# Moving the constant loads, the first bias addition and one group of scatters in an attention and mixture-of-experts kernel

## The reference

```
mod = (silu(c) @ wmod).reshape(4, 6, 1, 256); sa, ca, ga, sb, cb, gb = ...
h = layernorm(x) * (1 + ca) + sa
x = x + ga * attention(h)            # 16 heads of 16 channels, softmax over 1024 keys
h = layernorm(x) * (1 + cb) + sb
x = x + gb * ffn(h)                  # sigmoid gate, top 6 of 32 experts out of 4 of 8 groups,
                                     # silu(g) * u @ down per expert, plus one shared expert
```

## Time and profile before

| | us |
|---|---|
| median of 3 runs (lowest, highest) | 1454.37 (1452.69, 1455.62) |
| the profiled execution, its own time | 1454.37 |
| the profiled execution, span from first to last instruction | 1452.5 |
| attention with routing, about | 126 to 900 |
| TensorE busy | 1312.8 (90%) |
| VectorE busy | 1142.6 (79%) |
| GpSimd busy | 606.2 (42%) |

### The profile page before, as it was taken

One profiled execution on the slowest core, in us unless ns is written; L12 is line 12 of the kernel. 1 busy time (PEld: TensorE's weight loads), 2 busy tenths in 40 slices (PEclk: granted clock), 3 DMA queues, 4 the chain that ended last, 5 costly groups with the idle time before them and its releaser, 6 DMA issues.

```text
span 1452.5 us, 30593 instructions
## 1 busy us (share of the span) xinstructions
PE 1312.8 (90%) x8111; PEld 659.5 (45%) x8112; DVE 1142.6 (79%) x2793; ACT 754.2 (52%) x1155; POOL 606.2 (42%) x782
## 2 busy tenths in 40 slices
PE   7997999999999999999999998999999999999500
PEld 4552222333323323333233334657888888888400
DVE  7886999999999999999999972634666666566498
ACT  3772577767676676667676683103333333333100
POOL 4000123324634547346364477243555555555300
PEclk9997799999999999999999999999999999999855
DMA  6887355436345544465354647674555555555497
GB/s 219 262 267 189 114 164 131 103 82 135 99 118 151 130 109 105 116 160 125 88 127 136 185 130 222 213 236 125 175 178 172 180 179 169 181 176 171 167 418 299
DMA packets 216958, 243.52 MB, mean 168 GB/s; under 512 B 93949, under 2 KB 181501, under 8 KB 216738
## 3 DMA queue, kind: packets, MB, share of 16 engines
q1 hardware_dynamic: 187890, 164.78, 41.4%
q0 software_dynamic: 21776, 68.07, 13.1%
q10 hardware_dynamic: 7200, 9.51, 2.0%
HBM read 133.98 MB, written 108.28 MB: 167 GB/s over the span
## 4 chain that ended last, share of the span: by engine, by line
PE 68%; DVE 17%; DMA 3%; issue 1%; ACT 1%; SPq 1%; POOL 0%; DVEq 0%; POOLq 0%
PE ex_psGU L1620 14%; PE psO L1169 13%; PE psE L1156 12%; PE psM L1146 9%; DVE piece_max L1044 9%; PE ex_psY L1635 7%; PE ex_psX L1611 3%; PE psGU L1464 2%; PE psM L503 2%; PE psX L1475 2%; DVE wide L1758 2%; PE ex_psA L1629 2%; DVE wide L1760 2%; PE psM L522 1%; DVE wide L1761 1%
## 5 line engine op out<-in xcount | busy, mean ns | idle before, releaser
L1044 DVE TENSOR_REDUCE piece_max<-psM 128x1 f32<-128x512 f32 x1024 | 642.8, 682 | 26.4 <-PE psM L1146 22.9
L1110 ACT ACTIVATE wide<-psE 128x1024 f32<-128x1024 f32 x512 | 497.2, 1021 | 205.4 <-PE psE L1156 203.3
L1146 PE MATMUL psM<-wide 48*128 48x512 bf16 x1024 | 324.6, 395 | 19.7 <-DVE piece_max L1044 11.7
L1156 PE MATMUL psE<-wide 49*128 49x512 bf16 (+1 forms) x2048 | 330.1, 381 | 1.0 <-DMA wide<-maxima 0.5
L1704 POOL DMA_INDIRECT results<-vals_inv,places x223 | 213.7, 958 | 184.2 <-DVE vals_inv L1688 123.0
L1169 PE MATMUL psO<-wide 128*32 128x512 f32 x2048 | 274.0, 607 | 0.6 <-ACT wide L1110 0.6
L1146 PEld LDWEIGHTS psM<-wide 48*128 48x128 bf16 x1024 | 78.1, 93 | 348.0 <-DVE piece_max L1044 276.4
L1620 PE MATMUL ex_psGU<-wide,ex_xT 128*128 x892 | 231.8, 382 | 0.8 <-ACT ex_xT L1653 0.5
L1620 PEld LDWEIGHTS ex_psGU<-wide,ex_xT 128*128 128x128 f32 x892 | 152.0, 190 | 16.6 <-issue 4.6
L1156 PEld LDWEIGHTS psE<-wide 49*128 49x128 bf16 (+1 forms) x2048 | 117.7, 95 | 91.0 <-issue 9.4
L1653 ACT ACTIVATE ex_xT<-ex_psX 128x256 f32<-128x256 f32 x223 | 85.3, 383 | 122.9 <-PE ex_psX L1611 121.8
(11 more groups left out here) (240 smaller groups left out, 1222.0 us busy)
## 6 DMA issues: line engine op xcount, KB each, us to landing
wide<-qk_parts SPq DMA_DIRECT2D x384, 64.0 KB
wide<-results SPq DMA_DIRECT2D x16, 1536.0 KB, 10.5
rows<-lists SPq DMA_DIRECT2D x112, 160.0 KB, 2.2
last_rows<-lists SPq DMA_DIRECT2D x111, 160.0 KB, 2.7
qk_parts<-parts SPq DMA_DIRECT2D x32, 384.0 KB, 3.1
xin<-in_x_dram SPq DMA_DIRECT2D x16, 512.0 KB, 4.1
v_values<-vst SPq DMA_DIRECT2D x32, 256.0 KB, 3.6
wide<-v_values SPq DMA_DIRECT2D x16, 512.0 KB
```

Source lines behind the costliest of these rows:

```text
L1044: v.tensor_reduce(piece_max[:, qh, (x * PAIRS + h) * KT // QH + qt, kh:kh + 1], bank_of("piece", PIECES * group + n), AX.X, ALU.max, negat ...
L1110: nc.scalar.activation(probs[:, step % 2, 2 * pair:2 * pair + 2], psE[:, pair], ACT.Exp, scale=HD ** -0.5).then_inc(exp_ok, 1)
L1146: nc.tensor.matmul(bank_of(*user), qa[g][rows, h, qt * P:(qt + 1) * P], ka[g][rows, h, kh * 512:(kh + 1) * 512], start=True, stop=True).th ...
L1156: mm = nc.tensor.matmul(psE[:, pair, x], k[g][part, pair, kt * P:(kt + 1) * P], q[g][part, pair, qh * 512:(qh + 1) * 512], start=(q is qa) ...
```

## The change

There are three edits. On SP the constants and `load_x(0)` go ahead of the loop, and so ahead of `put_max(2)`. On GpSimd the wait for the constants, `scale_out(0)` and `add_bias(0)` go ahead of the 33 DMAs that fill the spare lists. In the odd chunks `add_bias(c + 1)` goes ahead of portion 2 of the scatters, as in the even ones.

```diff
@@ SP
             load_group(sp, env, 0, 3)
-            def load_constants():
-                for to, of in ((env.wo, env.woT), (env.gate_w, env.gateT), (env.wsg, env.wsgT), (env.wsd, env.wsdT)):
-                    sp.dma_start(to[:], of.rearrange("(k p) n -> p k n", p=P)).then_inc(const_in, 16)
-                sp.dma_start(env.bo_bc[:], env.bo_d.to_broadcast([P, D])).then_inc(const_in, 16)
-                sp.dma_start(env.ebias[:], env.ebias_d.to_broadcast([P, E])).then_inc(const_in, 16)
-
+            for to, of in ((env.wo, env.woT), (env.gate_w, env.gateT), (env.wsg, env.wsgT), (env.wsd, env.wsdT)):
+                sp.dma_start(to[:], of.rearrange("(k p) n -> p k n", p=P)).then_inc(const_in, 16)
+            sp.dma_start(env.bo_bc[:], env.bo_d.to_broadcast([P, D])).then_inc(const_in, 16)
+            sp.dma_start(env.ebias[:], env.ebias_d.to_broadcast([P, E])).then_inc(const_in, 16)
+            load_x(0)
...
                 if group + 1 < NGR:
                     put_max(2 * (group + 1))
-                if group == 0:
-                    load_constants()
-                    load_x(0)
                 if group % 2 == 0 and c >= 0:
                     load_x(c + 1)
@@ GpSimd
             pool.wait_ge(pads_built, 3)
+            pool.wait_ge(env.const_in, 16 * 6)
+            scale_out(0)
+            add_bias(0)
             spare = env.lists[E * CAP:LIST_ROWS].rearrange("(k p) n -> p k n", p=P)
             for k in range(E):
                 pool.wait_ge(summed, k + 1)
                 pool.dma_start(spare[:, k, 0:TARGET], env.pad_row[:, 0:TARGET]).then_inc(spare_in, 16)
             pool.dma_start(spare[:, :, TARGET:ROW], spare_to[:].bitcast(F32)).then_inc(spare_in, 16)
-            pool.wait_ge(env.const_in, 16 * 6)
-            scale_out(0)
-            add_bias(0)
...
                 if c % CPB:
                     scale_out((c + 1) // CPB)
-                    scatter_portion(c - 1, 2)
-                    add_bias(c + 1)
-                else:
-                    add_bias(c + 1)
-                    scatter_portion(c - 1, 2)
+                add_bias(c + 1)
+                scatter_portion(c - 1, 2)
```

## The result

The changed kernel takes 1471.11 us (median of 4 runs, 1469.10 to 1479.81) against 1454.99 for the kernel before on the same chip (4 runs, 1452.69 to 1455.81): the ratio is 1.0133, with an interval of 1.0101 to 1.0166. That ratio is more than the two medians give (1.0111), since it goes by all 29 executions of the changed kernel on record, whose mean is 1473.9. It is slower, by some five times as much as forecast (16 to 19 us against 3.4), and outside the range. The profiled execution took 1471.53 us, its span is 1469.5, so the 17.0 us of the span are what has to be found.

A forecast was written before the change was run, and what follows sets the result against it. PE and DVE, holding each other in attention, were taken to bound the kernel. From 1454.4 us, +2.1 for held-up maxima and +1.3 for a clock fall gave 1457.8 us, slower; range 1453.6 to 1461.5.

The forecast's parts named there:

- The odd chunks: GpSimd's addition and four scatters change places in three chunks: no wait appears, zero within 0.3 us each.
- a wait in an odd chunk: Sign in the profile after that would show the prediction wrong; no wait was expected there.
- Everything has the same spacing from group 2 on: Expected sign in the profile after: spacing from group 2 unchanged, all shifted by one amount.
- The hold-up of the maxima: Start of group 1: stores behind constants and x land later, PE starts at 198.8 instead of 196.67, +2.1 us.
- The upper bound of +6.0: Start of group 1: slowest case, constants take 8.2 us, then the stores' full 2.25 us, landing at 200.3.
- in the same queue: Start of group 1: 1.7 MB ahead of four 1 KB stores in SP's queue delays them.
- The clock behind it: After PE's 2.6 us pause at group 1 the clock falls, +1.3 us; zero to 2.6 possible.
- rival (c): Group 1's round held up in full and the clock low for longer: 1460 to 1463 us, chance 0.09.
- GpSimd's front: Scaling and addition ahead of the pads: pads go out from about 198 to 208, cost and gain zero.
- rival (d): The burst of pads makes DVE wait for the denominators, up to +2 us: 1459.8 us, chance 0.07.
- Rival (a): Group 1's maxima not held up, stores find room among the constants: 1454.4 to 1453.9 us, chance 0.22.
- (b): PE held up at group 1 but the clock stays: 1456.5 us, chance 0.15.

The follow-up runs named there:

- e2: The kernel before with only the odd-chunk edit (bias addition ahead of the scatters): 1472.33 us, ratio 1.0112 to the kernel before.
- e3: The kernel before with the odd-chunk edit, but one of the four scatters kept ahead of the addition: 1454.22 us, ratio 0.9994.
- e4: The kernel before with the odd-chunk edit and `neg_max` as a one-operand reduction: 1454.43 us, ratio 0.9989.
- e11: Both front edits on the kernel before, old odd-chunk order, the seven constants and x DMAs issued from GpSimd's queue: 1460.78 us, ratio 1.0045.
- e1: The changed kernel with the odd chunks back in their old order: 1459.8 us, ratio 1.0037 to the kernel before.
- e7: The kernel before with only GpSimd's front edit (scaling and addition ahead of the pads), on the slower chip: 1556.58 us, ratio 1.0009.
- e9: The kernel before with only x's 512 KB moved ahead of the maxima, constants left in place: 1455.13 us, ratio 0.9998.
- e12: The whole change, with constants and x issued ahead of group 1's loads and `neg_max` as a one-operand reduction: 1454.55 us, ratio 1.0003.
- e5: The kernel before with the odd-chunk edit and the bias addition split into four quarters, on the slower chip: 1563.8 us, ratio 1.0074.
- e8: Both front edits on the kernel before, old odd-chunk order, the seven DMAs issued ahead of group 1's loads, slower chip: 1553.8 us, ratio 1.0006.
- e6: The kernel before with only SP's edit (seven DMAs ahead of the maxima), on the slower chip: 1560.19 us, ratio 1.0042.

## Why the prediction was wrong

It said 1457.8 us and slower; measured are 1471.1. Step by step:

- **The odd chunks, priced at zero within 0.3 us, three times.** This is the step that failed. It asked whether somebody *waits* for the exchanged instructions (the scores of the gate stand behind both, x is there), and found nobody; that was right. It did not ask what runs beside them. VectorE's `neg_max` and the addition have no data in common, so no order of semaphores shows them together, and in the odd chunks the trace of before shows them apart. Measured: a hold of 2.08 us each, 6.2 in all, and with the falls of the clock behind them +10.7 us in the changed kernel's three places (5.0 + 3.6 + 2.1) and about +16 in e2. e3 and e4 each remove all of it. The rows to compare were there, the 0.22 us of chunk 0 among them: the addition moved by 5 us, and within those 5 us stood one VectorE instruction with two SBUF operands.
- **The clock there** was left out with the hold: a term that is zero has no fall behind it. The prediction did name the sign by which it would fail, a wait in an odd chunk; it is PE's 2.40 us. "Everything has the same spacing from group 2 on" failed with it.
- **The hold-up of the maxima, +2.1.** Mechanism right, size short: +3.0. PE's pause was 0.62 to 1.41 us in other runs with SP's old order, so the 0.54 us to which the term was added was the lowest of them. The reading was to start at 196.4 and did at 196.92, and PE started 2.51 us behind that instead of 2.36. The upper bound of +6.0 held. The reason, "in the same queue", was wrong in part (e11). The section of the Trainium skill that the prediction sets against the term, "Anatomy of one DMA", gives its 2.0 us for transfers that GpSimd issues; the stores here are SP's, and their last one took 4.37 us.
- **The clock behind it, +1.3.** It fell as forecast, but for twice as long: about +2.7. I had the longer fall as the upper bound of the term and in rival (c), not in the sum. Together the front cost 5.7 us in the profile and +5.4 in e1, against 3.4 forecast; by itself it would have come out at 1459.8, inside the range.
- **GpSimd's front, zero.** Right as far as e7 can tell (+0.09%, -0.22 to +0.39). The pads ran back to back from 198.79 to 207.9, as forecast (198 to 208), and no wait for the denominators appeared, so rival (d) falls.
- **Rival (a), small stores slip through**: falls, the last one took 4.37 us. (b), no fall of the clock: falls.

Open: why the clock also falls where no long pause precedes (steps 60 and 92 of the changed kernel, with no pause over 0.43 us in the microseconds before). The fall of the kernel before at 602 is there in the changed kernel too, in the same step, at 618.3 to 621.7; in e1 to e4 and e9 to e12 it is absent, and the step is 1.03 us shorter for it. So these short falls come and go from run to run and carry about 1 us each. Also why e5 costs some 8 us more than its holds.

## What to carry to other kernels

Before a GpSimd arithmetic instruction is moved, look in VectorE's timeline at everything between its old and its new place, and mark what reads two operands from SBUF: here such an instruction waited for GpSimd's to end, and a reduction over one operand that computes the same did not. Look at one-operand instructions as well, by their durations: the next section has one that was held. Don't issue a bulk load (here 1.7 MB) right ahead of a small round trip that PE waits for, whichever queue carries it. And price a pause of PE twice where PE bounds the loop: once by its length, and once by a fall of the clock behind it, which here cost 1 to 3 us, or nothing.

## What the runs showed of the hardware

- A held VectorE instruction shows as a long duration, without a wait: 2.26 us instead of 0.18, and 1.22 or 0.64 when GpSimd's instruction is half or a quarter as long. GpSimd's scatters held nothing: in the kernel before, a scatter runs from 529.95 to 530.90, and the `neg_max` that begins within it at 530.69 takes 0.18.
- Which VectorE instruction is held depends on both engines' instructions, and one operand is no safeguard. At the start of the kernel before, GpSimd fills memory with four `MEMSET`s. Beside them VectorE's `TENSOR_SCALAR` with one tensor operand takes 1.81 us (0.17 in its other seven calls), while a `TENSOR_TENSOR` with two different operands takes its usual 0.16 to 0.17:

```profile
9.01 7.36 POOL L259 MEMSET wide<- 32x2048 bf16 x4
```

```profile
10.88 1.81 DVE L108 TENSOR_SCALAR mean<-mean 128x4 f32<-128x4 f32 x1
13.59 0.17 DVE L119 TENSOR_TENSOR newton<-newton,var 128x4 f32<-128x4 f32 x1
```

- The kernel before took 1455 us on the chips of the result, of e1 to e4 and of e9 to e12, and 1555 on that of e5 to e8; the ratios of alike experiments agree (e6 +0.42% there, e1 +0.37% here).
- The clock fell at pauses of 4.53, 3.70, 3.57 and 3.03 us (group 1), at all three of about 2.4 us in e2 and at two of three in the changed kernel, once at 1.62 and in one of three cases at 1.37. In the third odd chunk of the changed kernel it stayed at 1.00 behind 2.40, and at group 1 it stayed there behind 1.51 (e8), 1.41 (e4) and 1.38 (e3).
